# Q, K and V projections: three native fp32 matmuls on the inputs as they are, in place of nine fp32r matmuls on high and low parts

## The reference

```python
q = _split_heads(input_graph @ Wq + bq)
k = _split_heads(input_graph @ Wk + bk)
v = _split_heads(input_graph @ Wv + bv)
scores = jnp.einsum('bhqd,bhkd->bhqk', q, k) / jnp.sqrt(HD)
scores = scores + beta * adj_e                 # adj_e = adj[:, None, :, :]
scores = jnp.where(adj_e > 0, scores, -9e15)
probs = jax.nn.softmax(scores, axis=-1)
out = jnp.einsum('bhqk,bhkd->bhqd', probs, v)
...
x = _layernorm(x + out)
```

## Time and profile before

| what | value |
|---|---|
| time, median of 3 runs | 877.06 us (875.73 to 879.56) |
| span of the profiled execution | 871.1 us |
| median time less that span | 6.0 us |
| granted TensorE clock, mean over the span | 0.990 of 2.4 GHz |
| TensorE matmul busy, its weight load | 748.6 us (86%), 657.1 us (75%) |
| VectorE, ScalarE, GpSimd busy | 643.6 us (74%), 632.8 us (73%), 420.7 us (48%) |
| DMA, mean | 128 GB/s |

### The profile page before, as it was taken

How to read it: one execution, slowest core, us unless ns; L and a number is a source line. 1 busy time by engine, 2 the same in 40 slices (tenths; PEclk the granted TensorE clock), 3 DMA queues, 4 the chain that set the end, 5 groups by cost and what they waited for, 6 DMA issues and landing times.

```text
span 871.1 us, 27397 instructions
## 1 busy us (share of the span) xinstructions
PE 748.6 (86%) x6528; PEld 657.1 (75%) x6528; DVE 643.6 (74%) x2487; ACT 632.8 (73%) x2116; POOL 420.7 (48%) x660
## 2 busy tenths in 40 slices
PE   5799998888988888989888989888998888999882
PEld 4678887777887777887777887777787777787761
DVE  3477777777777776877777787777877777787775
ACT  3477877777876777877777877777777777777772
POOL 1312555454555454556454556454456454456453
PEclk9899999999999999999999999999999999999997
DMA  4666444566544566544566545566544566544461
GB/s 151 140 140 140 104 119 117 137 158 155 107 118 114 137 157 156 107 117 116 133 158 157 109 119 116 129 157 158 116 118 114 124 158 157 115 118 113 96 147 36
DMA packets 59226, 111.87 MB, mean 128 GB/s; under 512 B 8704, under 2 KB 34560, under 8 KB 59136
## 3 DMA queue, kind: packets, MB, share of 16 engines
q1 hardware_dynamic: 59136, 111.05, 55.1%
HBM read 22.94 MB, written 12.58 MB: 41 GB/s over the span
## 4 chain that ended last, share of the span: by engine, by line
PE 35%; SPq 33%; DMA 18%; ACT 5%; issue 5%; DVE 3%; ACTq 0%; DVEq 0%
SPq L292 32%; PE j_bank L367 18%; DMA stack<-qk_parts 17%; PE t_bank L396 7%; PE s_bank L381 5%; PE o_bank L412 4%; ACT probs L472 2%; ACT qk_parts L486 2%; DVE qk_parts L567 2%; ACT probs_t L499 1%; PE o_bank L420 1%; DMA beta_col<-in_L_gnn_beta_dram 1%; ACTq L178 0%; PE j_bank L335 0%; DVE w_low L684 0%
## 5 line engine op out<-in xcount | busy, mean ns | idle before, releaser
L472 ACT ACTIVATE probs<-neg_scores,neg_max 128x256 f32<-128x256 f32 x768 | 381.9, 501 | 41.2 <-DVE neg_max L557 37.9
L557 DVE CUSTOM_DVE_ANT_0 neg_scores<-s_bank,bias_sb 128x256 f32<-128x256 f32 x768 | 290.2, 415 | 97.5 <-issue 51.6
L381 PE MATMUL s_bank<-stack 96*128 96x256 f32 x768 | 170.9, 304 | 95.5 <-DMA stack<-qk_parts 95.5
L396 PE MATMUL t_bank<-ident,probs 128*128 128x128 f32 x1536 | 231.4, 272 | 1.8 <-ACT probs L472 1.3
L381 PEld LDWEIGHTS s_bank<-stack 96*128 96x128 f32 x768 | 120.8, 190 | 125.5 <-issue 74.2
L396 PEld LDWEIGHTS t_bank<-ident,probs 128*128 128x128 f32 x1536 | 177.6, 141 | 3.3 <-ACT probs L472 1.8
L486 ACT ACTIVATE qk_parts<-j_bank,qk_bias 128x256 fp32r<-128x256 f32 x192 | 90.7, 473 | 120.6 <-PE j_bank L367 95.6
L577 DVE COPY probs_t<-t_bank 128x512 f32<-128x512 f32 x256 | 175.6, 686 | 1.1 <-PE t_bank L396 1.1
L567 DVE SCALAR_TENSOR_TENSOR qk_parts<-j_bank,qk_bias,qk_parts 128x256 fp32r<-128x256 f32 x192 | 92.4, 481 | 76.4 <-ACT qk_parts L486 76.4
L472 ACT ACTIVATION_READ_ACCUMULATOR probs<-neg_scores,neg_max 128x1 f32 x768 | 146.5, 191 | 0.0
L367 PE MATMUL j_bank<-xt_high,w_high 128*128 128x256 f32 x576 | 116.6, 311 | 6.0 <-ACT w_high L517 5.5
(11 more groups left out here) (59 smaller groups left out, 927.4 us busy)
## 6 DMA issues: line engine op xcount, KB each, us to landing
stack<-qk_parts SPq DMA_DIRECT2D x384, 192.0 KB, 4.0
x_sb<-in_x_dram SPq DMA_DIRECT2D x32, 384.0 KB, 4.9
out_dram<-o_sb SPq DMA_DIRECT2D x31, 384.0 KB, 4.5
adj_sb<-in_adj_dram SPq DMA_DIRECT2D x32, 256.0 KB, 4.8
w_raw<-in_L_gnn_Wq_dram SPq DMA_DIRECT2D x1, 576.0 KB, 4.2
w_raw<-in_L_gnn_Wk_dram SPq DMA_DIRECT2D x1, 576.0 KB, 6.6
w_raw<-in_L_gnn_Wv_dram SPq DMA_DIRECT2D x1, 576.0 KB, 8.2
out_dram<-o_sb SPq DMA_DIRECT2D x2, 192.0 KB, 2.0
```

The costliest lines, as they stand in the source:

```text
L381: mm = pe.matmul(b[:, t * N:(t + 1) * N], stack[0:R, par, 0, j, g, t * P:(t + 1) * P], stack[0:R, par, 1, j, g, :], start=True, stop=True)
L396: mm = pe.transpose(b[:, k * N + t * P:k * N + (t + 1) * P], probs[:, (T * h + t) % (T * NH), k * P:(k + 1) * P], ident[:, :])
L472: nc.scalar.activation(probs[:, slot, :], neg_scores[:, slot, :], ACT.Exp, bias=neg_max[:, par, t, h:h + 1], scale=-1.0, accum_out=row_sum ...
L557: nc.vector.tensor_tensor_reduce(neg_scores[:, (T * h + t) % (T * NH), :], s_bank[h % NS][:, t * N:(t + 1) * N], bias_sb[:, par, t, :], -1 ...
```

## The change

The high and low parts of x and of the weights go. ScalarE's copy of the transposed x stays, now as `x_t` in plain fp32, and a projection is three matmuls in plain fp32 on `w_raw` and `x_t`, one for each piece of the features. `xt_low`, `w_high` and `w_low` are no longer made; job 0 waits for ScalarE's copy of x where it waited for VectorE's low part. The split of the results (`qk_parts`), the stack, the scores and all the rest stay.

```diff
-    LOWS = 2 * G + C
+    LOWS = 2 * G
...
-        w_high = sb("w_high", [P, 3, C, D], F32R)
-        w_low = sb("w_low", [P, 3, C, D], F32R)
...
-        xt_high = sb("xt_high", [P, 2, C, N], F32R)
-        xt_low = sb("xt_low", [P, 2, C, N], F32R)
+        x_t = sb("x_t", [P, 2, C, N])
...
         def has_low(k):
-            return JOB[k][0] != "V"
+            return k < KV
...
                 if k == 0:
-                    wait(pe, low_ready, low_count(i, par, -1))
+                    wait(pe, high_ready, job_count(i, par, -1))
                 if k < KV:
                     q, g = k // G, k % G
-                    pairs = [(wp[:, q, c, g * P:(g + 1) * P], xp[:, par, c, :])
-                             for wp, xp in ((w_high, xt_high), (w_high, xt_low), (w_low, xt_high)) for c in range(C)]
+                    pairs = [(w_raw[:, q, c, g * P:(g + 1) * P], x_t[:, par, c, :]) for c in range(C)]
                     n = N
                 elif JOB[k][0] == "V":
                     t = JOB[k][1]
-                    pairs = [(xp[:, par, c, t * P:(t + 1) * P], wp[:, 2, c, :])
-                             for wp, xp in ((w_high, xt_high), (w_high, xt_low), (w_low, xt_high)) for c in range(C)]
+                    pairs = [(x_t[:, par, c, t * P:(t + 1) * P], w_raw[:, 2, c, :]) for c in range(C)]
                     n = D
...
                 for m, (w, a) in enumerate(pairs):
-                    if m == 2 * C:
-                        wait(pe, w_low_ready, weights_low)
                     mm = pe.matmul(b[:, 0:n], w, a, start=(m == 0), stop=(m == len(pairs) - 1))
...
-                if k == JOB.index((JOB[k][0], 0)) and JOB[k][0] != "X":
-                    pe.wait_ge(w_high_ready, 1 + "QKV".index(JOB[k][0]))
-                    project(0, 0, k, 1 + "QKV".index(JOB[k][0]))
-                else:
-                    project(0, 0, k)
+                if JOB[k] == ("Q", 0):
+                    pe.wait_ge(w_scaled, 2)
+                elif JOB[k] in (("K", 0), ("V", 0)):
+                    pe.wait_ge(w_in["QKV".index(JOB[k][0])], DMA)
+                project(0, 0, k)
...
-                else:
-                    ins = nc.vector.tensor_tensor(xt_low[:, 1 - par, JOB[k][1], :], b[:, 0:N],
-                                                  xt_high[:, 1 - par, JOB[k][1], :].bitcast(F32), ALU.subtract)
```

More of the change, by code:

```diff
@@ L138, in graph_attention_program @@
         w_scaled = sem("w_scaled")
-        w_high_ready = sem("w_high_ready")
-        w_low_ready = sem("w_low_ready")
         scores_ready = sem("scores_ready")
@@ L208, in low_count @@
                 done = -sum(has_low(n) for n in range(JOBS + k + 1, JOBS))
-            return count(i, par, LOWS, C + done)
+            return count(i, par, LOWS, done)
         def jobs_at(i, par, h):
@@ L341, in free_bank, with project @@
                 wait(pe, low_ready, low)
-            def project(i, par, k, weights_low=0):
+            def project(i, par, k):
                 b = j_bank[(C + par * JOBS + k) % 2]
@@ L492, in high @@
                 else:
-                    ins = nc.scalar.activation(xt_high[:, 1 - par, JOB[k][1], :], b[:, 0:N], ACT.Identity)
+                    ins = nc.scalar.activation(x_t[:, 1 - par, JOB[k][1], :], b[:, 0:N], ACT.Identity)
                 ins.then_inc(high_ready, 1)
@@ L509, in _ @@
                 act.wait_ge(job_ready, c + 1)
[L510 to L514, removed]
-                else:
-                    act.wait_ge(w_in[n], DMA)
-                nc.scalar.activation(w_high[:, n, :, :], w_raw[:, n, :, :], ACT.Identity).then_inc(w_high_ready, 1)
+                nc.scalar.activation(x_t[:, 0, c, :], first_bank[c][:, 0:N], ACT.Identity).then_inc(high_ready, 1)
             for k in range(JOBS):
@@ L564, in low @@
                 b = j_bank[(C + par * JOBS + k) % 2]
[L565 to L569, removed]
-                    ins = nc.vector.tensor_tensor(xt_low[:, 1 - par, JOB[k][1], :], b[:, 0:N],
-                                                  xt_high[:, 1 - par, JOB[k][1], :].bitcast(F32), ALU.subtract)
-                ins.then_inc(low_ready, 1)
+                q, g = k // G, k % G
+                nc.vector.scalar_tensor_tensor(qk_parts[:, par, 2 * q + 1, g, :], b[:, 0:N], qk_bias[:, q, g:g + 1],
+                                               qk_parts[:, par, 2 * q, g, :].bitcast(F32),
+                                               ALU.add, ALU.subtract).then_inc(low_ready, 1)
             def copy_turned(i, par, h):
@@ L676, in _ @@
             nc.vector.tensor_scalar(qk_bias[:, 0, :], qk_bias[:, 0, :], scale, None, ALU.mult).then_inc(w_scaled, 1)
[L677 to L688, removed]
             for k in range(JOBS):
-                if k == G:
-                    weights_low(2)
                 if k == KV:
```

## The result

The change made the kernel slower: 937.46 us (median of 3, 936.48 to 941.54) against 877.06, a ratio of 1.0705 (95% interval 1.067 to 1.074). The forecast was 912, range 904 to 930. The direction was right, and the time lies 25 us above the forecast and outside the range.

What follows compares the result with a forecast made beforehand. The prediction took each round as bound by TensorE's stretch up to job 5 plus the stack's DMAs; 35.7 us for longer jobs less 0.9 at the start took the span from 871.1 to 906, plus 6.0 gave 912 us, range 904 to 930.

Steps and rivals of the forecast that it cites:

- The sum of the jobs: Q and K jobs 1 to 5 on TensorE: 0.23 us more each over 31 rounds, 35.7 us added.
- The record of 0.215 us: Native fp32 matmul on TensorE: two records of 0.215 us each for 256 columns, so 1.29 us a job.
- the short rounds: Time per batch along the chain: forecast at 27.2 us for every round, against 26.0 before.
- the first stretch: Steps 0 to 4 with jobs 1 to 5, TensorE busy without a gap: added projection time lengthens the round in full.
- the rival that the added time is absorbed: ScalarE or VectorE ends the first stretch anyway, so longer jobs cost nothing: 877 us, chance 0.03.
- the 43 forecast: Sign of a right forecast: VectorE busy some 43 us less.
- The cover of the V jobs and job 0: While the stack's DMAs run: 0.99 us more a batch costs nothing, hidden under TensorE's waits of 3.1 us a batch.
- 65 were forecast: Sign of a right forecast: TensorE's waits for the stack fall from 95.5 to about 65 us.
- The removed work: VectorE's subtractions for x's low part (38.9 us) and the weights' splits on both engines: no gain counted.
- The start: Before the loop: projections begin without waiting for the weight split, so SP starts its first stack 0.9 us sooner.
- The one-round matmul: Rival on TensorE: a native matmul takes one round, a job 0.65 us, VectorE becomes the bound: 842 us, chance 0.05.
- the exposed weight load: Rival on TensorE: weight loads of 0.141 us stand between records, 0.85 us more a job: 1065 us, chance 0.05.

Runs made afterwards that it cites:

- e1: Changed kernel with three idle instructions put ahead of ScalarE's loop: 908.7 us, 1.0375 of the kernel before.
- e4: Kernel before with only the V jobs as native fp32 matmuls on the high parts: 893.3 us, ratio 1.021.
- e9: Kernel before without VectorE's subtractions for x's low part, the high part read in its place, same number of matmuls: 875.0 us, ratio 0.9979.
- e11: Kernel before (fp32r) with every job one step earlier and the mask made by GpSimd in place of VectorE: 849.2 us, ratio 0.9678.
- e8: Changed kernel (native fp32) with every job one step earlier and three idle instructions ahead of ScalarE's loop: 844.9 us, 0.9636 of the kernel before.
- e3: Kernel before with the Q and K jobs as three native fp32 matmuls on the high parts: 917.1 us, ratio 1.0473.
- e6: Kernel before with only the V jobs native and 180 idle instructions at the start of VectorE: 892.0 us, ratio 1.0182.
- e5: Changed kernel with two idle instructions put ahead of ScalarE's loop: 944.0 us, 1.0761 of the kernel before.

## Why the prediction was wrong

*The sum of the jobs* held. The record of 0.215 us was 0.217, the job 1.30, and the short rounds 27.2 us as written. Its 35.7 us are 32.9 in e1, where nothing else differs from the forecast's picture.

TensorE was again without a gap in the first stretch, 11.60 of 11.60 us busy from 457.40 to 469.00, which puts out the rival that the added time is absorbed. VectorE's busy time fell by 29.5 us (643.6 to 614.1) and not by the 43 forecast; nothing hangs on it.

*The cover of the V jobs and job 0* held in the changed kernel: e1 has rounds of 27.1 us, and waits for the stack of 61.4 us where 65 were forecast. But it held by luck of the same change. e4 shows that without the shorter VectorE code the V jobs cost 17.5 us, because the cover was already in use by VectorE's stretch, which stands in no row of the prediction; some half of the 17.5 is the lower clock behind eight of the turns.

*The removed work* is the step that failed. The prediction wrote of the weights' splits on both engines and of VectorE's subtractions, "I count no gain", and looked for what they cost nowhere but at the start. As work they were indeed worth nothing (e9). As instructions ahead of a loop they held ScalarE's loop in its place. Taking three out brought 26 stretches of 2.9 us; what stuck out is 27.5 us (60.4 less 32.9), by the rounds 13 turns of about 2.1 us, 1.7 us of it in one turn with the lower clock. That is the whole miss of 25 us and a little more.

*The start* was to be 0.9 us sooner and was 0.8 later (the first stack at 23.17 against 22.40): the data that VectorE's scaling waits for landed later in this execution. It is too small to matter.

*The rivals.* The one-round matmul and the exposed weight load are both out: six records of 0.217 us, while weight loads of 0.193 us (both in the groups shown above) run under them. The rule of the Trainium skill that a load overlaps only matmuls of other row groups ("TensorE: Matmul & The Clock Gate", The mechanism) is contradicted for native fp32 too; its four passes for fp32 ("FP8 and Floating Point Precision", TensorE Precision Notes) fit: two records of 0.217 us for 256 columns are some four cycles of 2.4 GHz a column.

What stays open: the exact rule by which VectorE's loop has its stretch or not. Nine instructions fewer (e11) left it and 24 fewer (e9, counted in the code: twelve ahead of the loop and twelve in it) removed it.

## What to carry to other kernels

Before costing an edit ahead of a loop, or inside one, at nothing, look at each engine's timeline at the loop's turn: in these kernels an idle time of ScalarE or VectorE there that waits for nothing went with packets of the kind `instruction`, so it was code being fetched. It can appear or vanish with a single instruction; the count of those packets and a few idle instructions are cheap tests for it. A wait that covers something may cover more than one thing, so list everything that ends under it before filling it. And where the chain alternates between one engine's stretch and a transfer, moving a job from the stretch to under the transfer was worth more (64 us between e1 and e8) than the form of the job (33 us between e1 and the kernel before).

## What the runs showed of the hardware

ScalarE's loop of this kernel turns without a stretch or with two, of 2.5 to 4.1 us each, depending on three instructions ahead of it; the second stretch stands between two neighbouring instructions, and with two idle instructions ahead of the loop it moved by two. VectorE's loop had one of about 4 us a turn, 4.6 at the longest (e3), and moved by 180 instructions two of at most 3.0 (e6). With stretches on one engine the program fetched 65 to 67 more packets of the kind `instruction` than with none, 14 of which it always had.

The Trainium skill ("Runtime: NRT & Kernel Launch", Instruction fetch mechanics) says that code is fetched in blocks into a small store, and that a taken branch to a block that is no longer there waits for a fetch. The runs agree: the packets come at the turns, and the sharp border between e5 and e1 looks like the edge of such a block. That ScalarE's two stretches are two blocks was not measured by itself.

TensorE's granted clock fell to 0.50 (1.2 GHz) behind eight of the 13 turns of e4, at the one shown after 0.90 us of work in 3.0; each such round took 1.0 to 1.3 us longer. The kernel before shows no such fall in its loop.

A native fp32 matmul of 128 stationary columns and 256 moving ones ran as two records of 0.217 us.

Idle instructions on VectorE cost about 0.1 us each (180 in 18.0 us, e6).
